# Gate and up of a gated feed-forward in two PSUM banks each, ternary even blocks, and one-hots built in pairs

## The reference, cut to what matters

```python
def _quantize_weight(w, group_size):            # group_size 128, over the 512 inputs
    wg = w.reshape(o, i // group_size, group_size)
    scale = jnp.mean(jnp.abs(wg), axis=-1, keepdims=True) + EPS
    wq = jnp.clip(jnp.round(wg / scale), -1.0, 1.0) * scale
...
gate = _bitlinear(x, w_gate)                     # 1408 hidden features
up = _bitlinear(x, w_up)
h = jax.nn.silu(gate) * up
return _bitlinear(h, w_down)
...
msg = h[src] * norm[:, None]                     # 100000 edges, sorted by dst
out = jax.ops.segment_sum(msg, dst, num_segments=N)
```

## Time and profile before

| | |
|---|---|
| time of the runs, median of 3 | 3543.81 us (3538.64 to 3545.29) |
| time of the profiled execution | 3537.91 us |
| its span, first to last instruction | 3536.2 us |
| mean granted PE clock over the span | 0.896 |
| busy: PE, PEld | 2806.9, 2050.4 us |
| busy: DVE, ACT, POOL | 1977.7, 1074.2, 2059.1 us |
| gate and up matmuls (hi, lo), line 1363 | 2464 and 1232 |

### The profile page before, as it was taken

The page is one execution under the profiler, slowest core; times in us unless marked ns, Lnnn a source line. Parts: engine busy times, 40 slices in busy tenths (PEclk is TensorE's granted clock), DMA queues, the critical chain, the costliest instruction groups (busy, mean ns, idle before and its releaser), DMA issues. The chain is left out here.

```text
span 3536.2 us, 58101 instructions
## 1 busy us (share of the span) xinstructions
PE 2806.9 (79%) x16521; PEld 2050.4 (58%) x16522; DVE 1977.7 (56%) x3616; ACT 1074.2 (30%) x1721; POOL 2059.1 (58%) x2157
## 2 busy tenths in 40 slices
PE   6855655213999999999999996778887878788799
PEld 6855544212788877787878886333333434335687
DVE  8888898966354545454454543433344344443676
ACT  3445555003233323323233323001121212223454
POOL 0077777767777777777700001777777777772454
PEclk9678778556999999999999998899999999998899
DMA  3222232002233333333322324777777877775564
GB/s 104 59 63 53 49 100 46 5 4 53 46 105 96 100 90 105 91 85 101 85 90 92 102 83 135 219 225 232 224 235 238 244 231 244 233 242 174 174 212 129
DMA packets 237217, 459.14 MB, mean 130 GB/s; under 512 B 80060, under 2 KB 102828, under 8 KB 236994
## 3 DMA queue, kind: packets, MB, share of 16 engines
q0 software_dynamic: 111360, 235.84, 25.8%
q1 hardware_dynamic: 125634, 220.46, 19.2%
HBM read 389.41 MB, written 73.25 MB: 131 GB/s over the span
## 5 line engine op out<-in xcount | busy, mean ns | idle before, releaser
L1814 POOL DMA_INDIRECT rows<-xn_rows,srcT x784 | 742.3, 947 | 273.1 <-issue 244.8
L122 POOL DMA_INDIRECT msg_c<-hid_rows,srcT x752 | 727.4, 967 | 244.1 <-issue 230.1
L1965 PE MATMUL pV<-rows,oh 128*128 x2240 | 554.9, 395 | 144.7 <-issue 49.6
L122 POOL DMA_INDIRECT msg_b<-hid_rows,srcT x464 | 455.0, 981 | 149.3 <-issue 137.7
L1965 PEld LDWEIGHTS pV<-rows,oh 128*128 x2240 | 223.8, 100 | 461.6 <-issue 290.2
L1388 PE MATMUL acc<-wd,hT 128*128 128x512 f32 x1617 | 399.6, 395 | 0.0
L1363 PE MATMUL pG<-xT,wgu_hi 128*128 128x512 f32 (+1 forms) x1232 | 373.1, 385 | 10.1 <-issue 8.4
L1363 PE MATMUL pU<-xT,wgu_hi 128*128 128x512 f32 (+1 forms) x1232 | 362.9, 376 | 0.0
L1388 PEld LDWEIGHTS acc<-wd,hT 128*128 128x128 f32 x1617 | 301.3, 188 | 67.9 <-issue 8.8
L2278 DVE SCALAR_TENSOR_TENSOR oh<-ids,bases,dstT 128x896 f32 x160 | 184.2, 1151 | 211.0 <-issue 145.4
L2266 DVE TENSOR_TENSOR agg<-agg,pV x161 | 110.2, 685 | 335.7 <-PE pV L1965 335.3
(11 more groups left out here) (393 smaller groups left out, 4549.7 us busy)
## 6 DMA issues: line engine op xcount, KB each, us to landing
wd<-wd_rows SPq DMA_DIRECT2D x154, 512.0 KB, 3.6
we<-in_L_ffn_expert_w SPq DMA_DIRECT2D x16, 1024.0 KB, 8.4
x_rows<-xr SPq DMA_DIRECT2D x49, 256.0 KB, 4.6
xn_rows<-pair SPq DMA_DIRECT2D x49, 256.0 KB, 2.0
rows<-xn_rows,srcT POOLq DMA_INDIRECT x784, 3.8
res<-x_rows SPq DMA_DIRECT2D x49, 256.0 KB
x_rows<-agg SPq DMA_DIRECT2D x49, 256.0 KB, 4.3
xt<-in_x SPq DMA_DIRECT2D x48, 256.0 KB, 2.7
```

What stands on the lines that cost most here:

```text
L122: nc.gpsimd.indirect_dma_start(msg[:, c, :], None, table, bass.IndirectOffsetOnAxis(ap=srcT[:, c:c + 1], axis=0)).then_inc(landed[u % 2], 16)
L1814: nc.gpsimd.indirect_dma_start(rows[:, u % RING, c, :], None, xn2_rows, bass.IndirectOffsetOnAxis(ap=srcT[:, u * Q + c:u * Q + c + 1], axi ...
L1965: last = nc.tensor.matmul(pV[:, ds(to, 1), :].rearrange("p a d -> p (a d)"), oh[:, ds(to, 1), c, :].rearrange("p a d -> p (a d)"), rows[:, ...
```

## The change

Of the four blocks of 128 inputs, blocks 0 and 2 are now called even, 1 and 3 odd. In stage B the even blocks of gate and up are left as -1, 0 and 1 and the odd ones are multiplied by the ratio of their scale to that of the even block ahead. So an even block is exact in its high part, and `wgu_lo` holds the odd blocks alone. The scale of each pair is a column of `wscale`.

In stage C gate and up are each computed in two banks, one for each pair of blocks, with five matmuls each. The four halves share three banks: gate's second has its own, up's second uses the bank of gate's first. ACT reads gate's first and up's second bank, scaled; DVE adds gate's second and up's first bank, scaled, in SBUF. The silu and the product read these sums. The low part has a place of its own, (f, 0.5). The bank in which the ids lay is given up: the ids are now bf16 numbers 0 to 127 in pairs in SBUF, and the first id of the tile is subtracted from the destinations. The one-hots are compared in bf16, in pairs of columns. The range of a tile is loaded at (f, 0.5), ahead of the low part, not in build. `scale_rows` moves from (1, 1) to (2, 0), and the four `rows` from (2, 0), (3, 0), (4, 0), (5, 0) to (3, 0), (3, 1), (4, 0), (4, 1).

```diff
-def build_unit(nc, dve, t, units_done, ranges, dstT, tiota, onehot, msg, rest, mstage, split, ready, used, msg_ready):
-
-    c0, units = tile_range(dve, ranges, t)
+def build_unit(nc, dve, c0, units, units_done, dstT, first, numbers, rel, onehot, msg, rest, mstage, split, related, ready, used, msg_ready):
...
-        nc.vector.tensor_tensor(onehot[:], bc(tiota.unsqueeze(1), (P, U, P)),
-                                bc(dstT[:, at].unsqueeze(2), (P, U, P)), ALU.is_equal).then_inc(ready, 1)
+        nc.vector.tensor_scalar(rel, dstT[:, at], first, None, ALU.subtract).then_inc(related, 1)
+        dve.wait_ge(related, n + 1)
+        full = (P, U // 2, P, 2)
+        nc.vector.tensor_tensor(onehot, bc(numbers.unsqueeze(1), full), bc(rel.rearrange("p (g j) -> p g j", j=2).unsqueeze(2), full),
+                                ALU.is_equal).then_inc(ready, 1)
...
-            last = nc.tensor.matmul(acc[j * HX:j * HX + H3, :], mstage[:, k, :], onehot[:, k, :], start=False, stop=False)
+            last = nc.tensor.matmul(acc[j * HX:j * HX + H3, :], mstage[:, k, :], onehot[:, k // 2, :, k % 2], start=False, stop=False)
...
-    first = {(FB - 1, 2): [(part.build, 0)]}
+    first = {(FB - 1, 0.5): [(part.prepare, 0)], (FB - 1, 2): [(part.build, 0)]}
...
+        (j, 0.5): [(part.prepare, j)] for j in (1, 2, 3)} | {
...
-    behind = {(2 + j, 0): [(part.rows, j)] for j in range(4)} | {
+    behind = {(3 + j // 2, j % 2): [(part.rows, j)] for j in range(4)} | {
...
-        (1, 1): [(part.scale_rows, None)]}
+        (2, 0): [(part.scale_rows, None)]}
...
             part.up(i, g, f)
+            beside(f, 0.5)
+            part.low(i, g, f)
             beside(f, 1)
```

Stage B on DVE:

```diff
-                    nc.vector.tensor_tensor(q[0], q[0], bc(scale.unsqueeze(2), full), ALU.mult).then_inc(done, 1)
...
+                    own.step(nc.vector.tensor_copy(wscale[:, at, :], even))
+                    own.step(nc.vector.reciprocal(sc[:, 1, 0:DK // 2], even))
+                    own.step(nc.vector.tensor_mul(sc[:, 2, 0:DK // 2], odd, sc[:, 1, 0:DK // 2]))
+                    odd_blocks = wq[:, j].rearrange("p (e b) c -> p e b c", b=2)[:, :, 1, :]
+                    nc.vector.tensor_tensor(odd_blocks, odd_blocks, bc(sc[:, 2, 0:DK // 2].unsqueeze(2), (P, DK // 2, P)),
+                                            ALU.mult).then_inc(s["wq"], 1)
```

The banks and PE in stage C:

```diff
-            pG = pb(ctx, "pG", [P, 4 * P], F32)
-            pU = pb(ctx, "pU", [P, 4 * P], F32)
+            pG = [pb(ctx, f"pGc{e}", [P, 4 * P], F32) for e in range(2)]
+            pU = [pb(ctx, "pU0", [P, 4 * P], F32), pG[0]]
...
-                    terms = [(w, v, c) for c in range(DK) for w, v in ((hi, x_hi), (hi, x_lo), (lo, x_hi))]
-                    for m, (w, v, c) in enumerate(terms):
-                        last = nc.tensor.matmul(ps[:, 0:n], w[:, c, :], v[:, c, :], start=(m == 0), stop=(m == len(terms) - 1))
+                    a, b = 2 * e, 2 * e + 1
+                    terms = ((hi[:, a, :], x_hi[:, a, :]), (hi[:, a, :], x_lo[:, a, :]), (hi[:, b, :], x_hi[:, b, :]),
+                             (hi[:, b, :], x_lo[:, b, :]), (lo[:, e, :], x_hi[:, b, :]))
+                    for m, (w, v) in enumerate(terms):
+                        last = nc.tensor.matmul(ps[:, 0:n], w, v, start=(m == 0), stop=(m == len(terms) - 1))
...
-                    wait_alone(pe, s["silu"], steps_before(i, g, f) + 1, s["fence_pe"])
-                    hidden(pG, i, g, f, 0).then_inc(s["gate_ps"], 1)
+                    wait_alone(pe, s["up_b"], step + 1, s["fence_pe"])
+                    hidden(pG[0], g, f, 0, 0).then_inc(s["gate_ps"], 1)
+                    wait_alone(pe, s["gate_b"], step + 1, s["fence_pe"])
+                    hidden(pG[1], g, f, 0, 1).then_inc(s["gate_ps"], 1)
...
-                    wait_alone(pe, s["hmul"], steps_before(i, g, f) + 1, s["fence_pe"])
-                    hidden(pU, i, g, f, 1).then_inc(s["up_ps"], 1)
+                    wait_alone(pe, s["up_a"], step + 1, s["fence_pe"])
+                    hidden(pU[0], g, f, 1, 0).then_inc(s["up_ps"], 1)
+                    wait_alone(pe, s["gate_a"], step + 1, s["fence_pe"])
+                    hidden(pU[1], g, f, 1, 1).then_inc(s["up_ps"], 1)
```

ACT in stage C:

```diff
-                    nc.scalar.activation(sil[:, 0:n], pG[:, 0:n], ACT.Silu).then_inc(s["silu"], 1)
+                    act.wait_ge(s["silu"], step + 1)
+                    act.wait_ge(s["gate_ps"], 2 * step + 1)
+                    nc.scalar.activation(gate_sum[:, 0:n], pG[0][:, 0:n], ACT.Identity, scale=wscale[:, f, 0:1]).then_inc(s["gate_a"], 1)
...
+                    nc.scalar.activation(up_sum[:, 0:n], pU[1][:, 0:n], ACT.Identity, scale=wscale[:, FB + f, 1:2]).then_inc(s["up_b"], 1)
+                    act.wait_ge(s["h_lo"], step + 1)
+                    act.wait_ge(s["gate_b"], step + 2)
+                    nc.scalar.activation(sil[:, 0:n], gate_sum[:, 0:n], ACT.Silu).then_inc(s["silu"], 1)
                     act.wait_ge(s["hmul"], step + 2)
```

DVE in stage C:

```diff
+                    nc.vector.scalar_tensor_tensor(gate_sum[:, 0:n], pG[1][:, 0:n], wscale[:, f, 1:2], gate_sum[:, 0:n],
+                                                   ALU.mult, ALU.add).then_inc(s["gate_b"], 1)
...
+                    nc.vector.scalar_tensor_tensor(up_sum[:, 0:n], pU[0][:, 0:n], wscale[:, FB + f, 0:1], up_sum[:, 0:n],
+                                                   ALU.mult, ALU.add).then_inc(s["up_a"], 1)
-                    nc.vector.tensor_tensor(sil[:, 0:n], pU[:, 0:n], sil[:, 0:n], ALU.mult).then_inc(s["hmul"], 1)
+                    nc.vector.tensor_tensor(sil[:, 0:n], up_sum[:, 0:n], sil[:, 0:n], ALU.mult).then_inc(s["hmul"], 1)
```

More of the change, by code:

```diff
@@ L310, with __init__ @@
 class Part:
-    def __init__(self, gate=nothing, up=nothing, down=nothing, build=nothing, sums=nothing, layer1=nothing,
+    def __init__(self, gate=nothing, up=nothing, low=nothing, down=nothing, prepare=nothing, build=nothing, sums=nothing, layer1=nothing,
                  stats=nothing, scale=nothing, norm=nothing, turn=nothing, residual=nothing, stats_rows=nothing, scale_rows=nothing,
@@ L316, in __init__ @@
                  enter=nothing, leave=nothing):
-        self.gate, self.up, self.down = gate, up, down
+        self.gate, self.up, self.low, self.down = gate, up, low, down
+        self.prepare = prepare
         self.build, self.sums, self.layer1 = build, sums, layer1
@@ L743, in program @@
         ffn = whole.enter_context(ExitStack())
-        wgu = [sb(ffn, f"wgu_{n}", [P, 2 * FB, DK, P], F32R) for n in ("hi", "lo")]
+        wgu_hi = sb(ffn, "wgu_hi", [P, 2 * FB, DK, P], F32R)
+        wgu_lo = sb(ffn, "wgu_lo", [P, 2 * FB, DK // 2, P], F32R)
+        wscale = sb(ffn, "wscale", [P, 2 * FB, DK // 2], F32)
         onehot = sb(ffn, "onehot", [P, U, P], BF16)
@@ L1171, in program @@
             "tail lanes ohs prod masked reduced parts far small_in nv_clear msg fence fence_sp fence_pe fence_dve onehot used split agg own_rows aggT conv relu "
-            "x1 var std rs xn xT_ps xT_hi xT_lo gate_ps up_ps silu hmul h_hi h_lo down x2 var2 std2 rs2 "
+            "related x1 var std rs xn xT_ps xT_hi xT_lo gate_ps up_ps gate_a gate_b up_a up_b silu hmul h_hi h_lo down x2 var2 std2 rs2 "
             "xn2 row_hi row_lo dve".split())}
@@ L1227, in program @@
             acc = pB_flat[:, 0:P]
-            tiota = pb(ctx, "tiles_c", [P, 512], F32)[:, 0:P]
+            first_id = sb(ctx, "first_id", [P, 1], F32)
+            numbers = sb(ctx, "numbers_c", [P, P, 2], BF16)[:]
+            rel = sb(ctx, "rel_c", [P, U], BF16)[:]
+            pairs = onehot[:].rearrange("p u n -> p (u n)").rearrange("p (g n j) -> p g n j", n=P, j=2)
+            gate_sum = sb(ctx, "gate_sum", [P, 4 * P], F32)
+            up_sum = sb(ctx, "up_sum", [P, 4 * P], F32)
             block = ctx.enter_context(nc.Block())
@@ L1305, in _ @@
             def _(pe):
-                for n in ("used", "silu", "hmul", "xT_lo"):
+                for n in ("used", "silu", "hmul", "xT_lo", "gate_b", "up_a", "up_b"):
                     pe.sem_inc(s[n], 1)
@@ L1336, in sums @@
                         wait_alone(pe, s["aggT"], T, s["fence_pe"])
-                    sum_columns(nc, pe, T, units_done, ranges, own_rows[:, j, :], mstage, identb, zerob, acc, onehot,
+                    sum_columns(nc, pe, T, units_done, ranges, own_rows[:, j, :], mstage, identb, zerob, acc, pairs,
                                 s["onehot"], s["used"]).then_inc(s["agg"], 1)
@@ L1488, in _ @@
                 own = Steps(dve, s["dve"])
-                own.step(nc.vector.tensor_copy(tiota, iota[:]))
+                own.step(nc.vector.tensor_copy(numbers, bc(iota[:].unsqueeze(2), (P, P, 2))))
+                own.step(nc.vector.memset(first_id[:], 0.0))
                 nc.vector.memset(w2b[:], 0.0)
@@ L1521, in build @@
                     nc.vector.tensor_copy(own_rows[:, j, :], own3[:, ds(T, 1), :].rearrange("p a b -> p (a b)")).then_inc(s["own_rows"], 1)
```

(6 more changed lines are left out.)

39 lines of the change are left out of this document (27 added, 12 removed).

## The result

The changed kernel takes 3484.64 us (median of 4 runs, 3476.32 to 3494.84), the kernel before on the same chip 3541.22 (3530.4 to 3545.29): a ratio of 0.985, 95% interval 0.9828 to 0.9871. Predicted were 3478 us. The profiled execution took 3487.15 us (span 3485.4), where 3473 were predicted.

A forecast was written before the change was run, and what follows sets the result against it. PE was taken to nearly set the feed-forward stage's time. Gains of 54 (six passes), 11.5 (last pass) and 4 (opening) gave 69, less 4 for the clock: 3537.91 - 65 = 3473 profiled, 3478 median, range 3425 to 3535.

The forecast's parts named there:

- What is removed.: Gate and up in the 894 to 2179 us stage: half of the wgu_lo matmuls go, 126 us of PE time.
- What is added.: Gate and up steps: ACT's scaled reads add 196 us, DVE's sums 208; a build falls from 5.9 us to 4.6.
- The group's end.: Last down of each group: PE waits 1.1 to 1.2 us for the low part, 14 ends, -17 us.
- The second link.: PE writes up's second bank only after ACT reads gate, queued behind DVE's late product; waits 2.3 us at most.
- The sizes of the groups.: Aggregation and feed-forward stage: gain 7 us per four-tile group, 2 per three-tile group, 4.5 in the last three-tile group.
- hand calculation: Three-tile group followed step by step: step 5 begins at 37.6 us against 38.4, end at 82.3 against 84.3.
- PE stays covered: Rival, feed-forward stage: all 126 us and the opening's 4 are gained, 3414 us; chance 0.13.
- The clock falls: slower: Rival, steps 1 to 6 of three-tile groups: waits halve PE's clock, 144 us lost, 3622 us; chance 0.09.
- the 4 us taken off for further falls: Feed-forward stage: three more falls of the clock were expected, 4 us off the gain of 69.
- No gain: Rival, tile builds: the range load is not hidden and delays the low part, 64 us, 3542 us; chance 0.09.
- The gathers: POOL's gathers coming late: 20.7 us a tile against PE's 24.9, 4 us of slack, no bound; no chance given.
- the weights' stage and the opening: Weights' stage: 2 us added, hidden before DVE's 18.4 us wait for gathers; opening: four builds, 4 us gained.

The follow-up runs named there:

- high-first run: Changed kernel with down's two high-part terms first for all tiles, the low-part wait only ahead of the last third: 3485.48 us, ratio 0.9826.
- six matmuls a bank: Changed kernel plus a sixth matmul in each bank, low part of the weights times low part of x: 3568.29 us, ratio 1.0077.
- a shorter build: Changed kernel with first-id subtraction and add moved into gaps and DVE's wait for the one-hots' end dropped: 3449.86 us, ratio 0.9742.
- plain one-hots: Changed kernel with one-hots built as before, f32 ids, no pairs, no first-id subtraction: 3528.95 us, ratio to before 0.9961.
- with four matmuls: Changed kernel with all matmuls of the weights' low part left out, so the output lacks it: 3436.99 us, ratio 0.9707.

## Why the prediction was right, and where it was not

**What is removed.** 616 matmuls went, and PE's busy time fell by 104 us in the stage, not 126. In three-tile groups it fell from 79.4 to 74.3 us (1550.92 to 1637.36 before, 1534.43 to 1620.69 after), 5.1 instead of 7.7. The clock is not the reason, since it is 0.98 in both. What the trace shows is that PE's work falls into more pieces: four matmuls in a row show 0.87 us, the same four behind a wait 0.94, and the end of the last matmul of a piece is no longer covered by the next. Inside that group PE pauses 9 times for over 0.2 us, where it paused 4 times before. That these pieces make up the whole 2.6 us is argued, not shown.

**What is added.** ACT's reads 0.689 and 0.580 us (0.69 and 0.58 said), DVE's sums 0.751 and 0.618 (0.75 and 0.60). The one-hots 1.492 (1.56). The build was put at 4.6 us and takes 4.0: of the issue time 7.7 us in 45 tiles are left, 0.17 each, not 0.5. The prediction cites the Trainium skill's perf-mode tier table (VectorE: DVE Perf Modes) for the rate. The trace agrees: broadcast in pairs the bf16 operation takes 1.492 us, where 2.818 was the slow one.

**The group's end.** 17 us said, 18.0 found, in 14 waits. The high-first run shows that these microseconds are nearly worthless to remove. The price in the sum was right as idle time; as a price in the kernel's time it was not: 12 us of it removed gave nothing.

**The second link.** It is there: PE waits 21.7 us for ACT's read of gate. One case, first PE, then ACT, then DVE:

```profile
1565.91 1.41 PE L1386 MATMUL pGc<-xT,wgu_hi 128*128 128x384 f32 x4 [2.03 <-ACT gate_sum L1486]
```
```profile
1563.23 0.52 ACT L1499 CAST hT<-sil 128x384 fp32r<-128x384 f32 x1 [1.21 <-DVE sil L1624]
1563.65 0.81 ACT L1513 ACTIVATE xn<-xr,small 128x512 f32<-128x512 f32 x1
1564.50 0.62 ACT L1516 CAST pair<-xn 128x512 f16<-128x512 f32 x1
1565.02 0.26 ACT L1452 COPY aggT<-pB 128x128 f32<-128x128 f32 x1
1565.18 0.58 ACT L1486 ACTIVATE gate_sum<-pGc,wscale 128x384 f32<-128x384 f32 x1
```
```profile
1558.74 1.49 DVE L173 TENSOR_TENSOR onehot<-numbers_c,rel_c 128x2560 bf16<-128x2560 bf16 x1
...
1562.64 0.56 DVE L1624 TENSOR_TENSOR sil<-up_sum,sil 128x384 f32<-128x384 f32 x1
```

The one-hots make the product late, the product the cast, and behind the cast row 1 and a copy stand ahead of the gate read: 2.03 us (2.3 said).

**The sizes of the groups.** This is the term that was mis-sized. Four-tile groups: 7 us said, 58.5 / 7 = 8.4 found. That mean hides three kinds. The group worked gave 7.3 (98.0 to 90.7) and the last one 7.9, the first of the stage 2.5, and the four at the start of a pass of the loop 10.2 each. In these four the kernel before idles twice on "issue", at the group's start and again after five matmuls, the 2.34 us in the earlier trace rows. The second pause, 7.8 us over the four, is in both kernels with gate in one bank and in none with gate in two, not even with six matmuls a bank. So it is not the shorter matmul work that removed it, and the prediction had no term for it; what did is open.

Three-tile groups: +2 in each of six and 4.5 in the last said; found are 5.7 us lost over the six and 3.4 gained in the last. In the group worked (1534.43 to 1620.69) step 5 begins at 36.7 (37.6 said), the wait in step 8 is 1.8 (2), and the group ends 83.5 us from its start before the loop's idle time (82.3 said, 84.3 before). In the group from 1354.76 the hand calculation misses a wait and what hangs on it:

```profile
1394.92 1.50 PE L1368 MATMUL pB<-w2b,aggT 128*128 128x512 f32 x2 [2.56 <-ACT aggT L1452]
1395.45 2.25 PE L1386 MATMUL pU<-xT,wgu_hi 128*128 128x384 f32 x4
```

The first layer waits for ACT's copy of the last tile's sums, which I had not put on ACT's queue, and behind it four matmuls take 2.25 us, where the same four at the same place take 1.27 at the higher level in the group worked: the step lasts 12.67 us, there 9.72. Two errors of opposite sign: the four-tile groups gave 9.5 us more than said and the three-tile groups 18.8 less. So 65.5 us, from which I had taken 4 for the clock, became 56.3. That the sum came out near was in good part luck.

**The rivals.** "PE stays covered" is out: a shorter build still gives the three-tile groups its whole length. "The clock falls: slower" was right in kind and small in size. The stage's granted clock is 0.98, as before, so the 4 us taken off for further falls are not found. Where the waits grow, though, the clock goes with them: 0.97 with plain one-hots, 0.96 with four matmuls. A single fall is cheap. The step with the wait of 2.03 us takes 10.29 us where the clock falls behind it (1560.87 to 1571.16, clock 0.83) and 9.10 where it does not (1381.26 to 1390.36, clock 1.00).

The Trainium skill (TensorE: Matmul & The Clock Gate, "A second HAM failure mode: psum-queue depth-cycling") tells of a kernel that cycles through PSUM banks and whose clock goes down and up between groups of matmuls. Here gate and up alone change bank four times in every step, and the steps shown lose the clock behind waits of 2.0 and 2.6 us, not at each change of bank.

"No gain" is out; in one respect it came near: matmuls and chain without the short one-hots give 0.4% (0.9961), the one-hots alone 0.55%, both 1.5%. **The gathers** are no bound, as said.

**The sum.** 65 us were said for the span, 50.8 came; 15.0 were lost by chance ahead of the gathers, and without them the change gives 66. By the medians of the pair it is 56.6. The forecast of the weights' stage and the opening (+2 hidden, -4) is met by -5.9. With paired one-hots alone that stretch is 718.4 us, as long as before, so the opening's 4 us are not shown to be theirs.

## What to carry to other kernels

Where two engines are both nearly busy, count by stage and by kind of step which of them sets the time: here an added matmul cost 0.8 of its length in one kind of group and 0.4 in the other, one taken away gave 0.5 and 0.2, and a shorter build counted in full in three-tile groups although PE was busy for 92% of the stage. Compare PE's busy time between kernels with the same matmuls as well: it shows what short waits cost beyond themselves. A change that lengthens a chain should come with one that takes work off the engine in front; here each alone brought under 0.6% and both 1.5%. Then look at the waits of an engine for its own results: two short operations moved into gaps and one such wait dropped brought another 32 us of the stage, where the one-hots alone had brought 24.
